# A scan kernel with experts on one core: one batch's convolution and ten chunks' softplus sums move to TensorE

## The reference

```
x = einsum('bld,ed->bel', hidden_states, in_proj_w)
xc = conv_general_dilated(x, conv_w, padding=[(3, 0)], feature_group_count=512)
x = silu(xc + conv_b[None, :, None])                    # called u in the kernel
x_dbl = einsum('bdl,ed->bel', x, x_proj_w)
dt_low, Bm, Cm = split(x_dbl, [16, 32], axis=1)
dt = softplus(einsum('brl,dr->bdl', dt_low, dt_proj_w) + dt_proj_b[None, :, None])
A = -exp(A_log)
state = state * exp(dt * A) + (dt * u) * B              # for each of 512 positions
y = sum over the 16 states of state * C, plus D * x, times silu(layernorm(z))
...
x = x + experts(layernorm(x)) + silu(h @ sw_gate) * (h @ sw_up) @ sw_down
```

## Time and profile before

| what | value |
|---|---|
| median of 3 runs | 1035.92 us (1034.25 to 1036.4) |
| the profiled execution | 1035.54 us, span 1033.8 us |
| busy in the span | PE 860.1 us (83%), DVE 601.4 (58%), POOL 565.3 (55%), ACT 500.3 (48%) |
| steps of batch 0, 1, 2, 3 | 126.0, 140.8, 143.7, 140.8 us |
| before the first scan; from the last batch's end to the first gather; from there on | 46.4; 38.6; 397.5 us |

### The profile page before, as it was taken

One profiled execution on the slowest core, in us unless ns is written; L12 is line 12 of the kernel. 1 busy time (PEld: TensorE's weight loads), 2 busy tenths in 40 slices (PEclk: granted clock), 3 DMA queues, 4 the chain that ended last, 5 costly groups with the idle time before them and its releaser, 6 DMA issues.

```text
span 1033.8 us, 12606 instructions
## 1 busy us (share of the span) xinstructions
PE 860.1 (83%) x4223; PEld 477.7 (46%) x4223; DVE 601.4 (58%) x859; ACT 500.3 (48%) x899; POOL 565.3 (55%) x318
## 2 busy tenths in 40 slices
...
GB/s 281 233 122 123 125 163 142 124 121 166 127 122 143 196 163 98 123 122 123 203 126 238 124 295 270 381 390 386 398 398 390 393 397 398 396 386 399 387 386 143
DMA packets 68412, 250.67 MB, mean 242 GB/s; under 512 B 10506, under 2 KB 13078, under 8 KB 68092
## 3 DMA queue, kind: packets, MB, share of 16 engines
...
## 4 chain that ended last, share of the span: by engine, by line
PE 49%; DVE 16%; DMA 12%; issue 6%; ACT 6%; SPq 3%; POOL 1%; POOLq 0%; DVEq 0%; ACTq 0%
PE ps L672 11%; PE ps L868 10%; DMA arena<-in_L_ffn_w_down 9%; PE ps L667 9%; PE ps L683 8%; PE ps L892 6%; DVE ps L1254 6%; DVE arena L1261 4%; SPq L562 3%; DVE arena L1280 2%; ACT ps L1063 2%; DVE arena L1254 1%; PE ps L901 1%; PE ps L780 1%; DMA xn_rows<-scores 1%
## 5 line engine op out<-in xcount | busy, mean ns | idle before, releaser
L1490 POOL TENSOR_TENSOR arena<-arena 128x1024 f32<-128x1024 f32 x128 | 300.0, 2361 | 57.4 <-DMA arena<-bc_rows 39.5
L667 PE MATMUL ps<-ident,arena 128*128 128x128 f32 (+2 forms) x1408 | 238.2, 321 | 84.6 <-DVE ps L1262 39.7
L667 PEld LDWEIGHTS ps<-ident,arena 128*128 128x128 f32 (+2 forms) x1408 | 199.3, 177 | 189.3 <-issue 84.4
L1063 ACT ACTIVATE ps<-arena,An 128x511 f32<-128x511 f32 x256 | 165.2, 680 | 109.2 <-DVE ps L1262 93.4
L1254 DVE TENSOR_TENSOR_SCAN ps<-ps,arena 128x1024 f32<-128x1024 f32 x82 | 187.6, 2288 | 15.5 <-ACT ps L1063 14.7
L868 PE MATMUL ps<-arena 128*64 128x352 f32 x984 | 161.8, 467 | 10.2 <-issue 6.5
L672 PE MATMUL ps<-xnT,sw 128*128 128x512 f32 x320 | 152.5, 621 | 12.7 <-ACT arena L1024 11.8
L1504 POOL DMA_INDIRECT arena<-xn_rows,idu x32 | 34.0, 1064 | 212.4 <-DVE wcol L1400 165.8
L1495 POOL TENSOR_TENSOR arena<-arena 128x1024 f32<-128x1024 f32 x46 | 108.3, 2355 | 49.6 <-DVE arena L1254 45.2
L1407 DVE TENSOR_TENSOR arena<-arena,ps 128x352 f32<-128x352 f32 x32 | 16.7, 522 | 175.3 <-PE ps L868 175.3
L868 PEld LDWEIGHTS ps<-arena 128*64 128x64 f32 x984 | 74.3, 138 | 84.9 <-issue 74.3
...
## 6 DMA issues: line engine op xcount, KB each, us to landing
arena<-bc_rows SPq DMA_DIRECT2D x128, 512.0 KB, 4.7
...
```

What stands on the lines that cost most here:

```text
L667: return nc.tensor.matmul(dst, src, ident[0:k, 0:k], is_transpose=True, **kw)
L1063: a = nc.scalar.activation(ps[:, 2 * (c % 2) + n, 1:L], dt[k][:, 1:L], ACT.Exp, scale=An[:, k, NB * g + n:NB * g + n + 1])
L1490: G.tensor_tensor(R[c % RING], dtu[k][:, None, :].to_broadcast([P, NB, L]), Brep[n % REPS], ALU.mult)\
```

## The change

`CONV_PE = (1,)`: for batch 1 the convolution is four products on PE for each chunk, with a diagonal matrix of one tap's weights as the stationary operand, accumulated in the bank of `inproj`. ACT copies `inproj` to SBUF (`acc`), makes the four diagonal matrices from the identity (`diag`, 16 instructions of 128x128 in all, one buffer `dg`), and applies Silu with the bias straight from PSUM. The twelve DVE instructions of that batch go.

`SUMS_PE = (1, 2)`: for chunks 2 and 3 of batch 0 and all chunks of batches 1 and 2 (ten chunks) dt is the sum of four tiles, made as four products with the identity (`sp` on PE). ACT writes 1 - w in place of w - 1, no longer corrects ln w, and instead evacuates the bank with that correction (`dt`). POOL's `c`, `sp` and `dt` of these chunks go; `dtu` stays.

`EXTRA` shrinks from 18 to 9 steps: nine even `weigh` move from DVE to POOL. The tables of places are written anew; the diff shows one line of each kind.

```diff
+CONV_PE = (1,)
+SUMS_PE = (1, 2)
...
-    "act xn_store": [39.99],
+    "act xn_store": [50.9],
...
-EXTRA = [0, 4, 6, 12, 18, 20, 24, 26, 36, 52, 56, 84, 88, 90, 100, 104, 116, 124]
+EXTRA = [0, 18, 24, 60, 84, 88, 104, 116, 124]
...
+        dg = sb("dg", [P, TAPS, P])
...
+        def sums_pe(b, c):
+            return b in SUMS_PE or b == 0 and c >= BYV
...
+                elif kind == "conv":
+                    claim(bank)
+                    pe.wait_ge(s["acc_ready"], i + 1)
+                    pe.wait_ge(s["dg_ready"], DC * CONV_PE.index(b) + c + 1)
+                    for j in reversed(range(TAPS)):
+                        d = TAPS - 1 - j
+                        mm = nc.tensor.matmul(ps[:, bank, d:L], dg[:, j, :], u[c][:, 0:L - d],
+                                              start=(d == 0), stop=(j == 0))
+                    mm.then_inc(s["conv_done"], 1)
+                    freed[bank] = [(s["u_ready"], i + 1)]
+                elif kind == "sp":
+                    claim(bank)
+                    pe.wait_ge(s["ln_ready"], i + 1)
+                    pe.wait_ge(s["xdt_ready"], i + 1)
+                    parts = (ex[c % 2], rest[c % 2], dtu[c], dt[c])
+                    for n, part in enumerate(parts):
+                        mm = nc.tensor.matmul(ps[:, bank, :], ident[:], part, start=(n == 0), stop=(n == len(parts) - 1))
+                    mm.then_inc(s["sums_mm"], 1)
+                    freed[bank] = [(s["dt_ready"], i + 1)]
...
+                elif kind == "diag":
+                    act.wait_ge(s["conv_done"], i)
+                    for j in range(TAPS):
+                        a = nc.scalar.activation(dg[:, j, :], ident[:], ACT.Copy, scale=cw[:, c, j:j + 1])
+                    a.then_inc(s["dg_ready"], 1)
...
+                elif kind == "dt":
+                    act.wait_ge(s["sums_mm"], pe_sums(i))
+                    nc.scalar.activation(dt[c], ps[:, BANK["sp", b, c], :], ACT.Identity, bias=neg_ln1[:])\
+                        .then_inc(s["dt_ready"], 1)
```

More of the change, by code:

```diff
@@ L91 @@
+    "dve xaggr": [37.88],
+    "act xnorm": [37.08],
+    "act xn": [38.08, 42.73, 45.74, 45.87],
+    "pe xnT": [42.85, 44.07, 44.84, 46.43],
+    "act xnT": [43.19, 45.69, 45.92, 45.94],
+    "pe logits": [43.01, 45.21, 46.51, 46.96],
+    "act xn_store": [51.07],
+    "pe sgate": [46.96, 47.46, 50.75, 51.43, 53.77, 54.33, 54.6, 54.75, 54.86, 55.25, 55.9, 56.81],
+    "dve top": [47.58],
+    "act negm": [46.59],
     "dve choose": [47.7],
     "act score": [47.88, 47.9, 47.91, 47.95],
-    "act norm": [49.81],
@@ L94 @@
[L94 to L96 removed]
+    "act norm": [48.03],
+    "act sc_store": [52.25],
+    "act scopy": [47.79, 52.24, 54.76, 54.92, 56.71, 57.01],
+    "pe pos": [48.47],
     "dve places": [49.24],
     "pool places": [49.77],
[L99 to L103 removed]
@@ L182 @@
     "act norm": [42.39],
-    "act sc_store": [42.47],
-    "act scopy": [42.29, 43.31, 48.04, 52.55, 53.9],
-    "dve places": [42.83],
+    "act sc_store": [43.41],
+    "act scopy": [41.91, 42.93, 47.66, 52.17, 53.52],
+    "dve places": [42.49],
     "pool places": [45.7],
     "dve hots": [44.15],
-    "act ohsid": [45.42, 45.75, 45.97, 47.23],
-    "pe table": [43.01, 43.67, 45.27, 45.8],
-    "dve table": [47.3],
+    "act ohsid": [45.8, 46.21, 46.36, 47.35],
+    "pe table": [43.01, 43.13, 43.67, 45.27],
+    "dve table": [47.04],
     "pe sel": [46.14],
     "dve ids": [47.79],
-    "dve ohsid": [44.62, 45.37, 45.44, 46.27],
+    "dve ohsid": [44.41, 45.16, 45.63, 46.06],
+    "pe inproj": [-25.68, -24.89, -24.49, -23.12],
+    "act acc": [-24.35, -24.18, -23.4, -23.24],
+    "dve conv": [-24.33, -24.26, -22.58, -22.29],
+    "act u": [-22.9, -22.26, -20.49, -20.29],
+    "pe xdbl": [-20.47],
 }
```

251 lines of the change are left out of this document (139 added, 112 removed).

## The result

The changed kernel takes 1063.09 us (median of 4 runs, 1061.5 to 1064.52) against 1035.09 us (1033.09 to 1036.4): ratio 1.0253, 95% interval 1.0228 to 1.0278. It is slower by 28 us as the medians have it and by 26 as the ratio has it, and outside the range of the prediction. Its profiled execution took 1062.1 us, span 1060.3, which is 26.6 over the profiled one of before.

What follows compares the result with a forecast made beforehand. No single engine was taken to bound the scans: DVE and POOL in batch 0, PE around the end of batch 1. Terms -1.0 - 1.5 - 1.0 + 3.0 + 6.9 + 1.0 + 3.0 = +10.4 gave about 1046 us, range 1024 to 1058.

Steps and rivals of the forecast that it cites:

- What bounds: Scan part: no single engine bounds it; DVE and POOL are busiest in batch 0, PE binds around the end of batch 1.
- three signs: Steps 56 to 71 about 7 us longer, PE over 95% busy; steps 8 to 15 ACT-released; gather 12 us after `sc_store`.
- Prices: Whole change: a sum 3.4 us at full clock, all products 48 to 99 us, diagonal matrices 6.0, table loads 1.28 each.
- Steps 0 to 15: Batch 0: steps 0 to 7 -3 us despite 3 us of waits; steps 8 to 15 +5 us through ACT's queue.
- Steps 48 to 71: Two sums on PE add 3.0 us in steps 48 to 55, two more add 6.9 us in steps 56 to 71.
- The next eight are unchanged: 0: Second eight steps of batch 1's first 16: no change in time, 0 us.
- No products are added: Steps 72 to 127: two `weigh` reach POOL while PE binds, +1.0 us (-3 to +4).
- the -1.5, -1.0, +3.0, +6.9 and +1.0: Terms in us for batch 0, batch 1's first 16 steps, steps 48 to 55, 56 to 71 and 72 to 127.
- Batch 1, first half: First 16 steps of batch 1: POOL loses six sums for one `weigh`, DVE is next; -1.0 us (-4 to +3).
- After the last step: Last step to first gather: the late `xn_store` delays the gather and shifts the rest, +3.0 us (0 to +9).
- The slower rival: Batch 0: products at half clock make PE a bound too, 133 us of PE in 126; 1059 us, chance 0.16.
- the faster rival: Batch 0 above all: DVE and POOL relief comes through, perhaps by a higher PE clock; 1024 us, chance 0.28.

Runs made afterwards that it cites:

- e8: Changed kernel with two products in place of four in each of the ten sums, so dt is a little off; ratio 1.0146.
- e1: Changed kernel with the second batch's convolution back on DVE and the ten sums still products; ratio 1.0199.
- e18: Changed kernel with the convolution on DVE at its old places and all ten sums still products; ratio 1.0237.
- e13: Kernel before with the new places of z, the new banks, and for batches 2 and 3 router, shared layer, loads and stores; ratio 1.0083.
- e12: Kernel before with only the changed kernel's nine offsets of a step; ratio 0.9944.
- e10: New order, convolution on DVE, of the products only the first batch's two sums, EXTRA with its 18 steps again; ratio 1.0256.
- e9: Changed kernel with only EXTRA put back to its 18 steps; ratio 1.0264.
- e17: New order without any product, EXTRA with 18 steps, and the second batch's convolution also at its old places; ratio 1.0182.
- e16: New order without any product, first batch's dt chain at its old places and engines, EXTRA with 18 steps; ratio 1.0201.
- the test of EXTRA: The 18 steps of EXTRA put back into the changed kernel (1.0264) and into e3 (1.0256); the new nine given to the kernel before (1.0109).
- e20: Kernel before with the changes of e12 and e13 together; ratio 1.0037.
- e14: Kernel before with the new dt chain places of batches 1 and 3 and the first batch's convolution placed as in the changed kernel; ratio 1.0009.
- e3: Changed kernel's order and new EXTRA, convolution on DVE, of the products only the sums of chunks 2 and 3 of the first batch; ratio 1.0277.
- e5: Changed kernel with the last batch's `xn_store` put back to its earlier place; ratio 1.0219.
- e6: Changed kernel with the four sums of the third batch back on POOL; ratio 1.0239.
- e19: e12 with the dt places of e14 and, of all products, only the four sums of batch 1; ratio 0.9957.

## Why the prediction was wrong

**What bounds.** Right as far as it went: no engine is full, batch 0 goes by DVE and POOL together, the end of batch 1 by PE. The row for steps 64 to 71 after (42.7 of 46.3 us) and the chain, nearly all PE from 289.91 to 355.88 us, continue:

```profile
322.80 1.93 PE ps L714 x16
324.72 1.02 PE ps L707 x8
325.75 3.44 PE ps L783 x8
329.18 0.87 PE ps L707 x8
330.06 5.35 PE ps L723 x12
...
349.20 3.43 PE ps L783 x8
```

Of the three signs that the prediction gave for being right two came: steps 56 to 71 are 8 us longer with PE busy 79.2 of 82.8 us, and in steps 8 to 15 the scans' longest releaser is ACT. The third missed narrowly: the first gather comes 11.6 us after `sc_store`'s issue, not 12, with the store of `xn` as its last wait. No sign looked at the stages that got new places and no product.

**Prices.** Right. A sum is 3.44 us at full clock (3.4 predicted), the 56 products take 45.6 + 16.6 = 62.2 us (48 to 99 predicted), sixteen diagonal matrices 5.1 us (6.0), the evacuation 0.684 (0.681):

```profile
L783 PE MATMUL ps<-arena,ident 128*128 128x512 f32 x80 | 45.6, 723 | 7.7 <-issue 5.7 <-DVE routes L1454 2.0
...
L1060 ACT ACTIVATE dg<-ident,cw 128x128 f32<-128x128 f32 x16 | 5.1, 392 | 2.3 <-PE ps L773 2.3
```

The row behind a table load starts 1.29 us after it, as in the earlier trace rows:

```profile
88.28 1.28 ACT L1071 ACT_TABLE_LOAD   x1
89.57 0.69 ACT L1071 ACTIVATE arena<-ps,vec 128x512 f32<-128x512 f32 x1
```

The drain of 1.38 us that the Trainium skill states (ScalarE: Activation LUTs, What ACT_TABLE_LOAD costs) is not in the trace here either: a load starts 0.02 us after the instruction ahead of it, and where nothing else is waited for the next instruction follows at its end.

**Steps 0 to 15: mechanism right, size too small.** The prediction put 3 us of waiting for the sums of chunks 2 and 3 into steps 0 to 7; ACT waited 6.5 us for the sums, and the scans 9.3 us for ACT, against 1.8 before. Changed kernel, steps 0 to 7 (who waits for whom: us in total, times, longest):

```profile
ACT arena L1126 <- PE ps L783: 6.5, 2, 4.3
DVE ps L1336 <- ACT ps L1145: 5.1, 1, 5.1
DVE arena L1336 <- ACT ps L1145: 4.2, 2, 2.5
```

With two products in place of four the first eight steps came to -4.3 (`e8`), beyond the predicted -3: the relief was real, and the sums' time on PE took it. In steps 8 to 15 the longest releaser of the scans is ACT, 16.6 us in all, against 0.2 before:

```profile
DVE ps L1336 <- ACT ps L1145: 9.7, 3, 6.2
...
DVE arena L1336 <- ACT ps L1145: 6.9, 2, 6.4
```

The stage is +8.8 in place of +5. By `e1`, 5.2 of it are the products of the convolution with their diagonal matrices and copies, the term as predicted. The other 3.6 are there without them; with the convolution's old places 0.6 are left (`e18`, whose steps 0 to 7 are longer instead), in which the moved Silu of z (+2.3 by `e13`) and the offsets (-2.4 by `e12`) cancel. The prediction had counted the table loads there and no other cost of the new places.

**Steps 48 to 71: the price was right, and it was not all.** Four sums were costed at 9.9 us; with the old EXTRA they cost 8.0 (`e10` to `e9`), and 13.8 came. The other 6 are there in `e10` and `e17`, which have no product in these steps.

**The step that failed** is the treatment of the rewritten tables of places. Eight table loads were priced, but only the two of steps 8 to 15 entered a term, and the late store is the only other cost that a new place got. Stages without a new product were left at what they took before: "The next eight are unchanged: 0", which held (-0.4), and "No products are added", +1.0 for steps 72 to 127. The new order without any product is 16.5 us longer in its steps than before (`e16`) or 18.6 (`e17`), and 1.0201 and 1.0182 times as long in the whole. From the changed kernel's 24.6 us this leaves 6 to 8 us for the products, where the terms had 8.4 (the -1.5, -1.0, +3.0, +6.9 and +1.0). The subtraction takes the two costs to add, which the test of EXTRA puts in doubt, so it does not prove each term; it says that most of what was missing was the move of the other work, which had been taken to be free.

**Where the order costs.** Against `e17`, `e20` has the old places of the statistics and the norm of x, router, shared layer, loads and stores for batches 0 and 1, of the dt chain of AT, and of three rows of the first batch's preparation. It is 17 us shorter in its steps, 15 of them behind step 48; against `e16` it is 15 us shorter, 11 of them there. The dt places with the first batch's rows cost 0.8 alone (`e14`), so the rest is left, by elimination; it was not tried alone, and that the dt places cost more in its company is not excluded. Four of the eight table loads are in it (`e13` and `e20` have the other four, and not all eight, as the text of `e13` says), 5.1 us of ACT. They stand in steps 56 to 63 and 88 to 95, which are only 1.1 and 1.6 us longer in `e17` than in `e20`, so the loads are a small part.

Behind step 48 DVE is busy 310.6 us in `e20` and 310.9 in `e16`, so the 11 us are idle time of DVE. The longest waits (total, times, longest), `e20` and then `e16`:

```profile
DVE arena L1319 <- PE ps L696: 9.7, 8, 2.9
DVE ps L1267 <- ACT ps L1076: 9.1, 6, 2.7
DVE hs L1314 <- PE ps L685: 3.7, 3, 1.7
```

```profile
DVE ps L1336 <- ACT ps L1145: 13.1, 8, 3.0
DVE arena L1388 <- PE ps L723: 12.2, 6, 4.4
DVE hs L1383 <- PE ps L712: 6.9, 6, 2.4
```

The scans (1267, 1336) wait some 6 us longer for ACT, 9.1 and 14.8 us with the scans that write to `R`; nearly as much more goes into DVE's own reads of what PE makes, the shared layer's result (1319, 1388) and hidden tiles (1314, 1383). Both queues, ACT's and DVE's, stand at evacuations. On ACT these are the copies of the hidden tiles; before, then `e20`, then `e17`:

```profile
L951 ACT COPY hs<-ps 128x512 f32<-128x512 f32 (+1 forms) x18 | 9.8, 543 | 7.9 <-PE ps L672 6.9 <-PE ps L674 1.0
```

```profile
L964 ACT COPY hs<-ps 128x512 f32<-128x512 f32 (+1 forms) x18 | 9.8, 544 | 10.5 <-PE ps L685 7.5 <-PE ps L687 3.0
```

```profile
L1010 ACT COPY hs<-ps 128x512 f32<-128x512 f32 (+1 forms) x18 | 9.8, 545 | 21.7 <-PE ps L712 19.7 <-PE ps L714 2.0
```

The same eighteen copies wait 7.9, 10.5 and 21.7 us for PE, 20.0 in `e16` and 21.8 in the changed kernel. While ACT stands at such a copy, `dA` of the next steps stands behind it. The prediction used this mechanism for the sums; here it acts on work whose place had moved and whose load had not. That these waits are the cause is read from the traces; no run moved the copies alone.

Part of the loss goes with the clock, a rival that no run separates. Steps 80 to 87, `e20` and then `e16`:

```profile
387.10:421.80 34.70, 26.02 (x140) 14.84 (x140) 32.83 (x42) 26.51 (x55) 29.52 (x18) 0.90 0.36 121
```

```profile
399.40:436.40 37.00, 29.65 (x144) 18.90 (x143) 32.93 (x44) 27.04 (x56) 30.43 (x19) 0.82 0.41 132
```

PE needs 3.6 us more for nearly the same records, at a granted clock of 0.82 in place of 0.90, and the stage is 2.3 us longer; steps 48 to 55 show the same (0.90 and 0.81). Whether the longer waits brought the clock down or the lower clock lengthened the waits stays open.

**Batch 1, first half** was forecast at -1.0 and came at +2.8; `e10`, `e16` and `e17` have +4.1 to +4.7 without products there, `e20` +2.6. The products took 1.3 to 1.9 us off this, and 3.2 against `e3` (+6.0), which has the new EXTRA too.

**After the last step**: +0.8 came. `xn_store` is the last wait, as predicted, but `e5` shows that it costs nothing; the +3.0 was no cost of the store.

**The rivals.** The slower rival (1059 us) was nearest in time and not in cause: PE is busy 91.7 us in batch 0, not 133, and at a mean clock of 0.80. The clock did rise, as the faster rival had it: 0.65 to 0.80 in batch 0. What it gave depended on who was last: in steps 0 to 7 a stretch at full clock was worth 1.7 us (`e6`), in steps 16 to 23 of `e19`, where DVE set the pace, nothing.

## What to carry to other kernels

On an engine with an in-order queue a moved instruction costs what stands behind it while it waits, not what it takes; a rewritten order is to be costed as a change of its own, first of all the evacuations that wait for another engine and stand ahead of the work on the critical path. Test it alone: the order without the new operations, and the operations' halves in the new order, price the two apart, as far as the costs add. Compare the granted clock of two stages before their lengths. Relief of one of two engines that are both within a microsecond of the stage's length buys nothing until the other is relieved too.

## What had not been expected

The nine offsets of a step, a by-product of the change, make the kernel before faster: 1030.77 us against 1037.06 beside it, ratio 0.9944 (0.9924 to 0.9964), with `weigh` one fifth of a step earlier and `dbu` a tenth. It has the lowest median of all versions; `e19` lies within its interval.

The steps as a whole repeat well where the clock does. Changed kernel and `e5` have the same order up to the last batch's end, and their scan parts are 569.6 and 569.9 us long; but the first scan starts at 45.8 and 49.9 us, and the part behind the first gather takes between 395.7 and 402.2 us over all kernels, though nothing in it was changed. Differences of 2 us in the whole say little. A stage of steps says more, once its clock has been compared.

TensorE's clock followed its load: the sums of batch 1, made there, raised the granted clock in steps 16 to 23 from 0.62 to 0.76 (the two rows of `e12` and `e19` above), with the length of the stage unchanged. The Trainium skill (TensorE: Matmul & The Clock Gate, What's actually happening) has activity release the throttle; the rows agree. The executions above with the same order show the other side: the same instructions were granted 1.00 in one and 0.96 in the other, and 0.90 and 0.81, so the clock of a stage is not fixed by its instructions alone.
